# Gather stage: VectorE's segment scans of a tile are issued ahead of the add for the tile three places back

## The chip, the cores and the metric

The kernel runs on 1 core of one Trainium2 chip. The metric is the device time of one execution in microseconds; lower is better. The times shown are the median of three runs and one profiled execution.

## The reference, cut to what matters

Two graph layers, each followed by a residual and a layer norm, over 50,000 nodes of 256 numbers with 12,500 edges sorted by destination. Layer 0 is the one in which the changed code works:

```python
h = einsum('ni,hid->nhd', x, W)
e = leaky(sum(h[src]*a_src) + sum(h[dst]*a_dst))
alpha_norm = softmax of e over the edges that share a dst
msg = alpha_norm[:, :, None] * h[src]
out_h = segment_sum(msg, dst)
x = layernorm(x + out_h.reshape(N, H*D) @ W_out)
```

Layer 1 does the same kind of thing with queries, keys, values and a gate, and ends in a second layer norm. A node that no edge points to gets nothing from either sum, so the kernel sends all nodes through a cheap path and redoes only the rows that edges touch.

## The kernel before, in words

All five engines run one list of steps in the same order (`order_of`). The list is a blend of two kinds of steps: *node* steps, 196 of them, each for 256 nodes without edges (class `Nodes`), and the steps of the edge stages, which follow each other: `Score`, a softmax, `Gather`, `Message`, a second softmax, `Output`. Each engine walks this list alone and waits on semaphores, so the list fixes the order of the work within each engine and nothing else.

The change is in `Gather`. The 12,500 edges are 100 tiles of 125. For tile n:

- GpSimd multiplies the stored head rows by the softmax weights into `MSG` (L1212), in step n-3.
- TensorE transposes both halves of `MSG` into PSUM bank 5 (L1247), in step n. Bank 5 is single, so this waits until the scans of tile n-1 have read it (`scanned`).
- VectorE runs two segment scans over bank 5 into `AT` (L1280), in step n. A scan takes its carry from the last column of tile n-1.
- TensorE multiplies `AT` by the output weights, four matmuls into bank 6 or 7 by turns (L1254), in step n+2. A bank is free again when the add of two tiles before has read it, which is the wait on `z_ready`.
- VectorE adds the bank to the residual row in `ring` (L1271), in step n+3, and counts `z_ready`.
- SyncE stores the row (L1223), in step n+4, and loads the row of a tile four ahead (L1232), and once in five tiles a mask (L1726).

TensorE's two waits of a step, with t the step and n = t - 2, are these:

```python
pe.wait_ge(self.made, t + 1)
at_least(pe, self.scanned, t)
...
pe.wait_ge(self.scanned, n + 1)
at_least(pe, self.z_ready, n - 1)
```

In the list the Gather steps share the time with 66 node steps, by turns: mostly one or two Gather steps between two node steps. Two Gather steps with no node step between them are called a *pair* below. From tile 4 on there are 36 pairs whose both tiles are live, the first with tiles 4 and 5, the last with tiles 96 and 97; steps 99 and 100 are a further pair in which only step 99 has scans, and steps 101 and 102 one with none.

A node step on TensorE is four transposes (L741) and eight matmuls (L751). On VectorE it is L770, L777, L785 and, in every second node step, the normalisation L791; in the others a tiny L764 stands in front and ScalarE normalises (L722). The second and third part of the first softmax's weights (L1175, L1177 on VectorE) are put in the list behind Gather steps 3 and 10.

Of the kernel before, what the change touches and what calls it, by code (L numbers as in the profile page):

```python
# [23 lines left out]
ALU = mybir.AluOpType  # L24
# [6 lines left out]
N, D = 50000, 256  # L31
# [4 lines left out]
EDGES, TILES = 125, 100  # L36
# [13 lines left out]
def at_least(eng, sem, value):  # L50

    if value > 0:
        eng.wait_ge(sem, value)
# [24 lines left out]
def live(s, lag, total):  # L78

    return 0 <= s - lag < total  # L80
# [77 lines left out]
class Head:  # L158
# [73 lines left out]
    def vector(self, dve):  # L232
        w = self.c.scratch
        dve.memset(w.row[:, 0:2, :], 0.0).then_inc(self.dve_done, 1)
        dve.memset(w.row[:, 2, :], float(SKIP)).then_inc(self.dve_done, 1)
        dve.memset(w.previ, -1).then_inc(self.dve_done, 1)
        dve.memset(w.nexti, -1).then_inc(self.dve_done, 1)
        dve.memset(w.row[:, 3, :], 1.0).then_inc(self.dve_done, 1)
        dve.wait_ge(self.dve_done, 5)
        dve.wait_ge(self.idx_in, 32)  # L240
        dve.tensor_copy(w.row[:, 0, 1:1 + EDGES], w.srci).then_inc(self.dve_done, 1)
        dve.tensor_copy(w.row[:, 1, 1:1 + EDGES], w.dsti).then_inc(self.dve_done, 1)
        dve.tensor_copy(w.dstf, w.dsti).then_inc(self.dve_done, 1)
        dve.wait_ge(self.dve_done, 8)
        dve.wait_ge(self.columns, 3)
# [935 lines left out]
class Gather:  # L1181
# [81 lines left out]
    def vector(self, dve):  # L1263
        c, ps, R = self.c, self.c.psum, self.c.R

        def emit(t):
            if live(t, 3, TILES):
                n = t - 3
                dve.wait_ge(self.product, n + 1)
                dve.wait_ge(self.rows_in[n % R], 16 * (n // R + 1))  # L1270
                dve.tensor_tensor(c.ring[:, n % R, 0, :], ps[:, 6 + n % 2, 0:D], c.ring[:, n % R, 0, :], ALU.add).then_inc(self.z_ready, 1)  # L1271
            if live(t, 0, TILES):
                if t % G == 0:
                    dve.wait_ge(self.keeps[t // G % 2], 16 * (t // (2 * G) + 1))
                dve.wait_ge(self.turned, t + 1)
                at_least(dve, self.product, t - 3)
                at_least(dve, self.scanned, t)
                for h in range(2):
                    carry = c.AT[:, (t - 1) % 4, h * P + EDGES:h * P + EDGES + 1] if t > 0 else 0.0
                    last = dve.tensor_tensor_scan(c.AT[:, t % 4, h * P:(h + 1) * P], c.MB[:, t // G % 2, t % G, :], ps[:, 5, h * P:(h + 1) * P], carry, ALU.mult, ALU.add)  # L1280
                last.then_inc(self.scanned, 1)
        return emit


# [660 lines left out]
```

## Time and profile before

| what | us |
|---|---|
| median of 3 runs | 1260.95 |
| lowest and highest run | 1257.87, 1261.74 |
| profiled execution, time | 1271.05 |
| profiled execution, span of the core | 1269.3 |
| TensorE busy, share of the span | 93% |
| VectorE busy, share of the span | 82% |
| Gather stage, from 445 to 706 us | 261 |

The span runs from the first to the last instruction of the profiled execution. Busy times are sums of instruction durations on an engine. TensorE's durations overlap from one matmul to the next and their ends are modelled, so TensorE is best read by the starts of its groups.

### The profile page before, as it was taken

How to read it: one execution, taken by the hardware profiler on the slowest of the kernel's cores; microseconds unless marked ns; L12 is line 12 of the kernel's file. 1: busy time of each engine (PE TensorE's matmuls, PEld its weight loads, DVE VectorE, ACT ScalarE, POOL GpSimd, SP SyncE). 2: the span in 40 equal slices, each digit the busy share in tenths (PEclk: the TensorE clock that was granted, in tenths of full speed). 3: DMA queues.
4: the chain of work that ended last, by engine and by line, in shares of the span. 5: the costliest groups of instructions: out<-in, count | busy, mean ns of one | idle time of the engine just before them, and what ended most of it. 6: DMA issues, size and time to landing. Idle time of an engine off the chain costs nothing.

```text
span 1269.3 us, 28496 instructions
## 1 busy us (share of the span) xinstructions
PE 1174.8 (93%) x6990; PEld 1024.3 (81%) x6990; DVE 1041.8 (82%) x3799; ACT 829.2 (65%) x2787; POOL 851.0 (67%) x1076
## 2 busy tenths in 40 slices
PE   2899999999998689999999899999999996899995
PEld 2788999988896578788788699989999995688884
DVE  2767776777778799999999889999999987788985
ACT  0366666665666866666666856666665668689996
POOL 6688888888883455555554677767677743278887
PEclk9899999999999899999999999999999998899998
DMA  7578888888884477788877787777777742555652
GB/s 210 164 224 284 270 268 257 270 268 266 262 265 132 134 254 249 244 267 249 259 253 238 220 255 217 217 223 221 206 220 223 224 136 78 158 189 187 185 188 96
DMA packets 208795, 276.99 MB, mean 218 GB/s; under 512 B 40044, under 2 KB 140419, under 8 KB 208633
## 3 DMA queue, kind: packets, MB, share of 16 engines
q1 hardware_dynamic: 187913, 223.83, 56.0%
q0 software_dynamic: 19264, 50.85, 13.5%
q8 instruction: 60, 0.98, 0.3%
q14 instruction: 102, 0.84, 0.2%
q10 hardware_dynamic: 1456, 0.49, 0.2%
HBM read 159.67 MB, written 117.12 MB: 218 GB/s over the span
## 4 chain that ended last, share of the span: by engine, by line
PE 58%; DVE 17%; issue 12%; POOL 7%; ACT 3%; DMA 1%; another core or an unknown queue 1%; SPq 1%; DVEq 0%; POOLq 0%; ACTq 0%
PE banks L751 19%; PE banks L864 7%; PE banks L741 6%; PE banks L1422 4%; POOL out L1577 4%; PE banks L854 3%; PE banks L1254 3%; POOL output_r L1583 3%; DVE AT L1280 3%; PE banks L866 2%; PE banks L1409 2%; PE banks L1427 2%; PE banks L953 2%; PE banks L1247 2%; DVE node_X L777 2%
## 5 line engine op out<-in xcount | busy, mean ns | idle before, releaser
L751 PE MATMUL banks<-m_ext,node_XT 128*128 128x257 f32 x1568 | 376.0, 382 | 0.0
L751 PEld LDWEIGHTS banks<-m_ext,node_XT 128*128 128x128 f32 x1568 | 284.6, 192 | 33.0
L777 DVE SCALAR_TENSOR_TENSOR node_X<-banks,node_be,node_X 128x256 f32<-128x256 f32 x392 | 169.4, 474 | 79.5 <-ACT node_be L703 53.6
L678 POOL TENSOR_TENSOR node_r<-node_vv,half 128x4 f32<-128x4 f32 (+1 forms) x202 | 212.8, 1053 | 17.1 <-POOL node_vv L673 0.3
L709 ACT ACTIVATE node_XT<-banks 128x512 f32<-128x512 f32 x196 | 117.5, 599 | 131.7 <-PE banks L741 126.9
L673 POOL TENSOR_SCALAR node_vv<-node_mv 128x4 f32<-128x4 f32 (+1 forms) x202 | 56.5, 279 | 190.3 <-DVE node_mv L785 173.7
L716 ACT ACTIVATE node_sq<-node_X 128x256 f32<-128x256 f32 x392 | 158.0, 409 | 1.2 <-DVE node_X L777 1.2
L770 DVE BATCH_NORM_STATS2 node_st<-node_X 128x6 f32<-128x256 f32 x392 | 145.4, 412 | 1.3 <-issue 0.5
L690 ACT ACTIVATE node_X<-node_X,node_r 128x256 f32<-128x256 f32 x326 | 146.0, 497 | 0.0
L741 PE MATMUL banks<-ident,node_X 128*128 128x128 f32 x784 | 122.0, 279 | 19.0 <-issue 11.9
L831 POOL DMA_INDIRECT ring<-in_x,src_col x100 | 106.8, 1068 | 26.5 <-issue 14.4
L877 ACT ACTIVATE ST<-banks 128x512 f32<-128x512 f32 x100 | 59.8, 598 | 97.5 <-PE banks L854 40.1
L1345 POOL DMA_INDIRECT ring<-rows,src_pos x100 | 106.2, 1062 | 22.8 <-issue 19.7
L741 PEld LDWEIGHTS banks<-ident,node_X 128*128 128x128 f32 x784 | 95.7, 148 | 31.9 <-issue 16.4
L831 POOL DMA_INDIRECT ring<-in_x,dst_col x100 | 97.0, 970 | 31.4 <-issue 31.1
L1577 POOL DMA_INDIRECT out<-store,last_col x90 | 91.4, 1015 | 23.7 <-issue 23.4
L864 PE MATMUL banks<-wh,ST 128*128 128x260 f32 x400 | 105.9, 387 | 1.5 <-ACT store L886 0.2
L1622 PE MATMUL banks<-m_ext,AT 128*128 128x257 f32 x400 | 106.2, 388 | 0.7 <-ACT AT L1660 0.5
L1422 PE MATMUL banks<-w_kv,ST 128*128 128x256 f32 x400 | 105.0, 385 | 0.3 <-DVE store L1470 0.3
L1254 PE MATMUL banks<-wo,AT 128*128 128x256 f32 x400 | 103.0, 380 | 0.0
L1280 DVE TENSOR_TENSOR_SCAN AT<-MB,AT,banks 128x128 f32<-128x128 f32 x198 | 84.0, 466 | 20.2 <-PE banks L1247 17.1
L1449 ACT ACTIVATE ST<-banks 128x512 f32<-128x512 f32 x100 | 59.3, 593 | 62.9 <-PE banks L1409 54.9
(270 smaller groups left out, 2740.8 us busy)
## 6 DMA issues: line engine op xcount, KB each, us to landing
node_X<-in_x SPq DMA_DIRECT2D x196, 256.0 KB
out<-node_X SPq DMA_DIRECT2D x196, 256.0 KB
ring<-rows SPq DMA_DIRECT2D x210, 128.0 KB
rows<-ring SPq DMA_DIRECT2D x100, 256.0 KB
rows<-ring SPq DMA_DIRECT2D x200, 128.0 KB
MB<-keeps SPq DMA_DIRECT2D x40, 320.0 KB, 4.5
store<-rows SPq DMA_DIRECT2D x90, 128.0 KB
MB<-picks SPq DMA_DIRECT2D x50, 128.0 KB
```

Of the source, the lines that this page charges most:

```text
L678: pool.tensor_tensor(r[:, s % 4, NT * lo:NT * hi], v, self.c.half[:, NT * lo:NT * hi], ALU.pow).then_inc(self.roots, 1)
L690: last = eng.activation(row, row, ACT.Identity, scale=rz)
L716: last = act.activation(self.sq[:, k, :], X[:, n % U, k, :], ACT.Square, scale=1.0 / D ** 0.5, accum_out=self.mv[:, s % 4, 1, k, 1:2])
L741: last = pe.transpose(ps[:, 4, k * D + h * P:k * D + (h + 1) * P], self.X[:, n % U, k, h * P:(h + 1) * P], c.ident[:, :])
L751: last = pe.matmul(ps[:, NT * o + k, 0:D + 1], self.XT[:, o, k * D + h * P:k * D + (h + 1) * P], c.m_ext[:, h, :], start=(h == 0), stop=(h ...
L770: last = dve.bn_stats(st[:, s % 2, k, :], X[:, s % U, k, :])
L777: last = dve.scalar_tensor_tensor(out=X[:, n % U, k, :], in0=ps[:, b + k, 0:D], scalar=self.be[:, n % 4, k:k + 1], in1=X[:, n % U, k, :], ...
L831: pool.indirect_dma_start(out=c.ring[:, n % R, side, :], out_offset=None, in_=self.x, in_offset=bass.IndirectOffsetOnAxis(ap=col[:, n:n + ...
L864: pe.matmul(ps[:, 6, 0:HP], c.ST[:, o, h * P:(h + 1) * P], c.wh[:, h, :], start=(h == 0), stop=(h == 1))
L1254: last = pe.matmul(ps[:, 6 + n % 2, 0:D], c.AT[:, n % 4, h * P:(h + 1) * P], c.wo[:, h, :], start=(h == 0), stop=(h == 1))
L1422: pe.matmul(ps[:, 6, 0:2 * DM], c.ST[:, o, h * P:(h + 1) * P], c.w_kv[:, h, :], start=(h == 0), stop=(h == 1))
L1577: pool.indirect_dma_start(out=self.out, out_offset=bass.IndirectOffsetOnAxis(ap=c.last_col[:, n:n + 1], axis=0), in_=self.row(n), in_offse ...
```

## The change

In each Gather step VectorE issued the add for tile t-3 and then the two scans of tile t. Now it issues the scans of tile t and then the add for tile t-3. Waits go with their instructions. No other engine's code is touched, and no instruction is added or removed.

```diff
         def emit(t):
-            if live(t, 3, TILES):
-                n = t - 3
-                dve.wait_ge(self.product, n + 1)
-                dve.wait_ge(self.rows_in[n % R], 16 * (n // R + 1))
-                dve.tensor_tensor(c.ring[:, n % R, 0, :], ps[:, 6 + n % 2, 0:D], c.ring[:, n % R, 0, :], ALU.add).then_inc(self.z_ready, 1)
             if live(t, 0, TILES):
                 if t % G == 0:
                     dve.wait_ge(self.keeps[t // G % 2], 16 * (t // (2 * G) + 1))
...
                 last.then_inc(self.scanned, 1)
+            if live(t, 3, TILES):
+                n = t - 3
+                dve.wait_ge(self.product, n + 1)
+                dve.wait_ge(self.rows_in[n % R], 16 * (n // R + 1))
+                dve.tensor_tensor(c.ring[:, n % R, 0, :], ps[:, 6 + n % 2, 0:D], c.ring[:, n % R, 0, :], ALU.add).then_inc(self.z_ready, 1)
         return emit
```

## Rows read from the trace of the kernel before

**Rows 1.** Page, the span and busy time by engine, with share and instructions.

```profile
span 1269.3 us, 28496 instructions
...
PE 1174.8 (93%) x6990; PEld 1024.3 (81%) x6990; DVE 1041.8 (82%) x3799; ACT 829.2 (65%) x2787; POOL 851.0 (67%) x1076
```

**Rows 2.** Busy time by stretch: start:end and length, the engines, clock, DMA share, GB/s.

```profile
445.00:706.00 261.00, 251.36 (x1347) 209.21 (x1348) 239.65 (x773) 170.53 (x562) 137.01 (x221) 1.00 0.79 249
```

**Rows 3.** Waits from 445 to 706: us in total, times, longest us.

```profile
DVE AT L1280 <- PE banks L1247: 17.1, 59, 0.5
PE banks L1247 <- DVE AT L1280: 9.6, 37, 1.3
```

**Rows 4.** Timeline, 560 to 575: start, us, instruction, idle before and releaser.

```profile
567.46 0.38 PE L1247 MATMUL banks<-ident,MSG 128*128 128x128 f32 x2
567.88 0.85 DVE L1280 TENSOR_TENSOR_SCAN AT<-MB,AT,banks 128x128 f32<-128x128 f32 x2 [0.45 <-PE banks L1247]
568.55 0.60 PE L741 MATMUL banks<-ident,node_X 128*128 128x128 f32 x4
568.65 0.73 DVE L770 BATCH_NORM_STATS2 node_st<-node_X 128x6 f32<-128x256 f32 x2
570.72 0.38 PE L1247 MATMUL banks<-ident,MSG 128*128 128x128 f32 x2
570.85 0.42 DVE L1271 TENSOR_TENSOR ring<-banks,ring 128x256 f32<-128x256 f32 x1
571.18 0.84 DVE L1280 TENSOR_TENSOR_SCAN AT<-MB,AT,banks 128x128 f32<-128x128 f32 x2
572.01 0.42 DVE L1271 TENSOR_TENSOR ring<-banks,ring 128x256 f32<-128x256 f32 x1
572.17 0.41 PE L1247 MATMUL banks<-ident,MSG 128*128 128x128 f32 x2 [0.20 <-DVE AT L1280]
572.41 1.03 PE L1254 MATMUL banks<-wo,AT 128*128 128x256 f32 x4
572.67 0.85 DVE L1280 TENSOR_TENSOR_SCAN AT<-MB,AT,banks 128x128 f32<-128x128 f32 x2 [0.24 <-PE banks L1247]
573.28 0.60 PE L741 MATMUL banks<-ident,node_X 128*128 128x128 f32 x4
```

**Rows 5.** Timeline behind step 10, where the softmax part stands in VectorE's queue.

```profile
470.32 1.63 DVE L1175 RECIPROCAL scores<-scores 128x240 f32<-128x240 f32 x1
...
476.34 0.41 PE L1247 MATMUL banks<-ident,MSG 128*128 128x128 f32 x2 [1.26 <-DVE AT L1280]
```

**Rows 6.** Timeline, VectorE, scans and add in the first and last of 36 pairs.

```profile
453.54 0.84 DVE L1280 TENSOR_TENSOR_SCAN AT<-MB,AT,banks 128x128 f32<-128x128 f32 x2
454.30 0.40 DVE L1271 TENSOR_TENSOR ring<-banks,ring 128x256 f32<-128x256 f32 x1
...
692.41 0.85 DVE L1280 TENSOR_TENSOR_SCAN AT<-MB,AT,banks 128x128 f32<-128x128 f32 x2 [0.40 <-PE banks L1247]
693.27 0.42 DVE L1271 TENSOR_TENSOR ring<-banks,ring 128x256 f32<-128x256 f32 x1
```

**Rows 7.** Timeline near 1094, Output stage: matmuls that had waited for VectorE.

```profile
1093.85 0.48 DVE L1702 SCALAR_TENSOR_TENSOR ring<-banks,output_gates,ring 128x256 f32<-128x256 f32 x1
1094.45 0.73 PEld L1622 LDWEIGHTS banks<-m_ext,AT 128*128 128x128 f32 x4 [0.47 <-issue]
1094.48 1.11 PE L1622 MATMUL banks<-m_ext,AT 128*128 128x257 f32 x4 [0.26 <-DVE ring L1702]
1095.42 0.27 PE L1640 MATMUL banks<-ident,MSG 128*128 128x128 f32 x1
```

**Rows 8.** Timeline near 1050, Message stage: the same kind of wait.

```profile
1050.24 0.29 DVE L1470 TENSOR_TENSOR store<-banks,S 128x128 f32<-128x128 f32 x1 [2.63 <-ACT S L1456]
...
1050.63 1.10 PE L1422 MATMUL banks<-w_kv,ST 128*128 128x256 f32 x4 [0.34 <-DVE store L1470]
...
1051.57 0.38 PE L1423 MATMUL banks<-we,MB 128*128 128x128 f32 x2
```

**Rows 9.** Timeline, the end of the scans, steps 99 and 100.

```profile
700.17 1.89 PE L1254 MATMUL banks<-wo,AT 128*128 128x256 f32 x8
700.38 0.85 DVE L1280 TENSOR_TENSOR_SCAN AT<-MB,AT,banks 128x128 f32<-128x128 f32 x2 [0.43 <-PE banks L1247]
701.90 0.60 PE L741 MATMUL banks<-ident,node_X 128*128 128x128 f32 x4
```

**Rows 10.** SyncE's queue, waits from 445 to 706 us.

```profile
SPq L1223 <- DVE ring L1271: 46.3, 38, 3.4
```

**Rows 11.** DMA issues by line, 500 to 650: KB each, median us to landing.

```profile
MB<-keeps SPq DMA_DIRECT2D x11, 320.0 KB, 4.4
```

## The prediction, written before the result was known

> **What bounds the kernel now.** I began with the page [rows 1]: TensorE is busy for 93% of the span and VectorE for 82%, over stages that differ, so neither number says what the changed step is worth. The changed lines run only in the Gather stage, and I took the busy times of that stretch alone [rows 2]. In its 261 us TensorE is busy for 251.4 (96%) and VectorE for 239.7 (92%), at a granted clock of 1.00. Nearly everything that makes TensorE later there makes the stage longer.
>
> Then the waits of the stage [rows 3]. TensorE waits for one thing only: its transposes of MSG (L1247) for the scans (L1280), 37 times, 9.6 us in total. VectorE waits 59 times, 17.1 us, for those transposes. TensorE never waits at L1254, the matmul that needs the bank which the add empties. So z_ready is a wait that is always satisfied today.
>
> The timeline shows where the 37 waits are [rows 4]. A transpose at 567.46 belongs to a Gather step that stands alone between node steps. VectorE waits for it and starts the scans at 567.88, 0.42 later; TensorE goes on with the node step at 568.55 and loses nothing. The transposes at 570.72 and 572.17 are a pair. The second can't start before the scans at 571.18 have ended, at 572.02, and starts 0.15 behind them. A pair without any wait would take 1.09 us from transpose to transpose (567.46 to 568.55 is one step's work); it takes 1.45. Counting from the end e of the first tile's scans, the pair runs: second transposes e + 0.15, matmul L1254 e + 0.39, second scans e + 0.65, next node step on TensorE e + 1.26. The last figure is 1.25 to 1.27 in 31 of the 36 pairs.
>
> **The change part by part.** Nothing is added or removed: 100 adds of 0.41 and 100 pairs of scans change places. VectorE's busy time stays. What can move is who waits, and there are three questions.
>
> *Do the scans start earlier?* In a step that stands alone, no: they wait for TensorE already [rows 4], so there the add moves from an idle place to one behind the scans. In a pair behind a node step with the normalisation L791, VectorE is late and the add stands directly ahead of the scans (570.85, then 571.18), 0.33 us that seem to be gained. But the add of the step before now stands ahead of that node step. From scans to scans, 567.88 to 571.18, VectorE's work is scans 0.77, node step 2.20 (568.65 to 570.85), add 0.33, together 3.30; afterwards it is scans 0.77, add 0.33, node step 2.20, again 3.30. And the transposes at 570.72 wouldn't have let the scans start before 571.14. The gain per pair is 0; if the order did matter, 0.04. The stretch with the softmax part [rows 5] is the same case: until TensorE is released at 476.34 VectorE has the same work in another order.
>
> *Does TensorE get a new wait?* Yes, in each pair. In the second step t + 1 of a pair TensorE's matmul for tile t - 1 needs the add of tile t - 3. That add was issued ahead of the scans of tile t, for which the transposes had to wait anyhow. Now it is issued behind them. What I read as its new end is where the second add of a pair ends today, for it too follows the scans directly: 572.01 + 0.42 = 572.43, e + 0.41 [rows 4]; over the 36 pairs the median is 0.41, from 0.32 in the first pair to 0.45, with 0.43 in the last [rows 6]. The matmul would like to start at e + 0.39, and its weight load before that, so it waits.
>
> What a released group of four such matmuls costs must come from elsewhere, since L1254 has never waited. In the Output stage L1622, four matmuls of 257 columns, waits for an add of VectorE that ends at 1094.33; the weights start at 1094.45, the matmul at 1094.48, and what follows on TensorE at 1095.42, 1.09 after the release [rows 7]. In the Message stage the same is 1050.53 to 1051.57, 1.04 [rows 8]. The first has the same shape of wait (an add that reads PSUM and ends a bank's use), and I take 1.09. The node step behind a pair then starts at e + 0.41 + 1.09 = e + 1.50 in place of e + 1.26: **0.24 us per pair**. The bounds are 0.32 + 1.04 - 1.26 = 0.10 and 0.45 + 1.09 - 1.26 = 0.28. The second scans stay at e + 0.65, since the add ends before that, so nothing is won or lost there.
>
> The weights of the released group are loaded at 1094.45, 0.12 after the add's end and not before it [rows 7]. If they could be in place when the release comes, the group would run at the pace of an undisturbed one, 0.87 (572.41 to 573.28), from 0.15 behind the release (572.02 to 572.17): 0.41 + 0.15 + 0.87 - 1.26 = 0.17 per pair. The Trainium skill, "TensorE: Matmul & The Clock Gate", section "Architectural detail: the array is 16× 32×32, not 1× 128×128", says that TensorE's queue can pull weight loads ahead of matmuls in flight, which would make for the smaller price. The load at 1094.45 shows no such thing over a wait, so I keep 0.24.
>
> *How many, and do they add up?* There are 36 pairs. The one at steps 10 and 11 costs nothing, as TensorE afterwards stands 1.26 us for VectorE anyway [rows 5]. 35 x 0.24 = 8.4 us. They add, as the next step after each pair is paced by TensorE: its transposes come 2.17 behind the node step's start (568.55 to 570.72) and the scans 0.42 behind that, e + 1.50 + 2.17 + 0.42 = e + 4.09, while VectorE with the add now ahead of the node step is ready at e + 0.65 + 0.77 + 0.33 + 2.20 = e + 3.95 at the worst. Today these are e + 3.85 and e + 3.95. 13 pairs come directly after another pair's node step, and where that step holds L791, VectorE was the later one by up to 0.10, so part of the delay is hidden. With about half of them, 0.1 x 6 = 0.6 comes off; most second scans start at 0.60 rather than 0.65, and I take off 0.3.
>
> *The end.* Steps 99 and 100 have their eight matmuls back to back, from 700.17, with the node step at 701.90 [rows 9]. The four of step 100 need the add of tile 96, which now follows the scans that end at 701.23: 701.23 + 0.41 + 1.09 = 702.73, 0.83 later than today, once. Steps 101 and 102 have no scans.
>
> *Other engines.* SyncE waits 38 times for the add before it stores the row [rows 10], and behind the store in its queue are the row load, the mask load and the node steps' transfers. All of these go out later by the scans, about 0.8 us. The loads are issued four node steps (some 16 us) or four tiles (some 10 us) ahead, and a mask takes 4.4 us to land [rows 11]: hidden. If that cover were gone, it would be one shift of 0.8 us, not one per tile, as the queue keeps its pace. GpSimd and ScalarE wait for no add.
>
> Sum: 8.4 - 0.3 + 0.83 = 8.9 us on the profiled execution's span of 1269.3 (its time is 1271.05), 0.7%. That execution is 10.1 us slower than the median of the runs shown, 1260.95, and I assume the same 8.9 there: **1269.9 us**. A change of 0.3%, 3.8 us, is about what a measurement of this kernel can tell from none.
>
> **The rivals.**
>
> *Faster: the scans were held by the add.* If VectorE were late by the whole add in every pair behind an L791, with no add taking its place ahead of the node step, some 20 pairs would each gain 0.33, 6.6 us: 1254.4. For it speaks the order of 570.85 and 571.18, and 9.6 us of TensorE waiting for scans. Against it, the same 3.30 us of work either way, and the transposes that allow 0.04. It decides only if the matmul's wait is also satisfied by e + 0.27, that is an add end at e + 0.15, and the earliest seen is 0.32. Chance 0.07.
>
> *No change: the new wait is absorbed.* If VectorE and not TensorE sets when the next scans of a pair start, a delay of TensorE up to its slack is given back. I found up to 0.10 of such slack, and in pairs after pairs only; a run without profiling might have more. With all pairs at the lower bound, 35 x 0.10 + 0.5 = 4 us is still at the edge of what can be told. If two thirds of the 8.9 are absorbed: 1264. Chance 0.13.
>
> *Slower than forecast: SyncE's late queue.* If transfers of the node steps or masks lose their cover in places, VectorE stands at L770 or L1280. By the 0.8 us it would have to happen several times, each behind a fresh catching up: five times is 4 us, 1274. SyncE has had waits of up to 3.4 us for the add [rows 10] without anyone waiting for a load. Chance 0.08.
>
> *Slower by less: the released group loses no pace.* At 0.17 per pair and 701.23 + 0.41 + 0.15 + 0.87 - 701.90 = 0.76 at the end, the sum is 35 x 0.17 - 0.3 + 0.76 = 6.4: 1267.4. Against it stand both rows of released groups [rows 7, 8], whose groups take longer than an undisturbed one: 1094.48 to 1095.42 and 1050.63 to 1051.57 are 0.94 each. Chance 0.07. The rule cited above would lead here.
>
> *My forecast,* 35 new waits of 0.10 to 0.28, has the remaining 0.65.
>
> **How the numbers follow.** The bounds give 35 x 0.10 + 0.5 = 4 and 35 x 0.28 + 0.9 = 10.7 us: 1265 to 1271.7. The measurement itself moves by 2 or 3 us (1257.87 to 1261.74 in three runs), and the upper rival reaches to 1274. The range 1264 to 1274 leaves out the faster rival and part of the absorbed case below, and little above. Slower by over 0.3%: the forecast, the smaller price and the upper rival, 0.80, with 0.02 from the absorbed case at its edge, make 0.82. Within 0.3%: 0.11. Faster: 0.07.
>
> **What the changed profile would show.** The waits of the stage would have a new row, L1254 for the add L1271, some 36 times with about 0.1 us each, and perhaps 0.5 at the end. The transposes L1247 wait for the scans as often as before and for about the same total. In the timeline of a pair the node step stands at e + 1.50, not 1.26; the scans, at most 0.04 earlier. The stage lasts about 270 us in place of 261, with TensorE's busy share a little lower. VectorE's idle time ahead of the scans grows. I would be wrong if the L1247 wait shrank by several us, if L1254 never waited, or if the node steps stood later but the stage didn't.

## The result

| kernel | median us | runs |
|---|---|---|
| before | 1259.45 (1256.98 to 1261.74) | 20 |
| changed | 1264.86 (1261.68 to 1266.97) | 20 |

The ratio is 1.0036, with a 95% interval of 1.0028 to 1.0045: the changed kernel is 3.5 to 5.7 us slower. The direction was forecast and the time lies in the range, but the loss was forecast at 8.9 us; the medians differ by 5.4 us, and 1.0036 is 4.5 us, about half of the forecast.

The two profiled executions can't be compared by their spans: the changed kernel's is 1260.4 us, 8.9 us *shorter* than the kernel before's 1269.3 [rows 1]. The first transposes of MSG begin at 441.0 us in one and at 431.2 in the other, and up to there the two kernels run the same instructions; in the other nine profiles of this document they begin at 429.8 to 432.8 us, so it is the kernel before's profile that stands out. Behind the stage the changed kernel's profile is 4.3 us shorter too (559.9 us for 564.2), at a granted clock of 0.98 for 0.97. So I compare the stage: from the first transposes of MSG to the start of the last add. The page of the changed kernel, its span and engines:

```profile
span 1260.4 us, 28496 instructions
...
PE 1172.6 (93%) x6990; PEld 1019.6 (81%) x6990; DVE 1041.0 (83%) x3799; ACT 835.3 (66%) x2787; POOL 851.2 (68%) x1076
```

Busy time by stretch, kernel before, from the first transposes to the last add (columns as in [rows 2]):

```profile
441.00:705.10 264.10, 253.41 (x1359) 210.59 (x1358) 241.26 (x775) 174.11 (x573) 139.31 (x226) 1.00 0.79 250
```

The same stretch of the changed kernel:

```profile
431.20:700.50 269.30, 258.48 (x1359) 211.44 (x1358) 240.65 (x775) 174.29 (x573) 141.32 (x226) 1.00 0.79 246
```

The stage is 5.2 us longer, which lies within the 3.5 to 5.7 us that the times give: it is as large as the whole loss. VectorE's busy time is the same to 0.6 us (240.65 for 241.26). The waits from 435 to 700 us in the changed kernel, the answer to [rows 3]:

```profile
DVE AT L1275 <- PE banks L1247: 21.7, 57, 0.6
PE banks L1247 <- DVE AT L1275: 9.2, 37, 1.3
...
PE banks L1254 <- DVE ring L1281: 0.5, 1, 0.5
```

TensorE's waits hardly moved, and the new wait shows once only, with 0.5 us. The waits within the 36 pairs are not in this view: TensorE's busy time grew by 5.1 us instead. A group of two transposes is shown as 0.41 us long, with a modelled end, and the matmul that waits starts before that end. So the wait is read from the starts. The timeline of the changed kernel, the answer to [rows 4]:

```profile
559.65 0.38 PE L1247 MATMUL banks<-ident,MSG 128*128 128x128 f32 x2
560.07 0.85 DVE L1275 TENSOR_TENSOR_SCAN AT<-MB,AT,banks 128x128 f32<-128x128 f32 x2 [0.57 <-PE banks L1247]
560.84 0.40 DVE L1281 TENSOR_TENSOR ring<-banks,ring 128x256 f32<-128x256 f32 x1
...
562.91 0.38 PE L1247 MATMUL banks<-ident,MSG 128*128 128x128 f32 x2
563.37 0.84 DVE L1275 TENSOR_TENSOR_SCAN AT<-MB,AT,banks 128x128 f32<-128x128 f32 x2
564.13 0.40 DVE L1281 TENSOR_TENSOR ring<-banks,ring 128x256 f32<-128x256 f32 x1
564.36 0.41 PE L1247 MATMUL banks<-ident,MSG 128*128 128x128 f32 x2 [0.20 <-DVE AT L1275]
564.64 0.73 PEld L1254 LDWEIGHTS banks<-wo,AT 128*128 128x128 f32 x4
564.67 1.10 PE L1254 MATMUL banks<-wo,AT 128*128 128x256 f32 x4
564.86 0.85 DVE L1275 TENSOR_TENSOR_SCAN AT<-MB,AT,banks 128x128 f32<-128x128 f32 x2 [0.33 <-PE banks L1247]
565.61 0.60 PE L741 MATMUL banks<-ident,node_X 128*128 128x128 f32 x4
```

With e = 563.37 + 0.84 = 564.21: transposes e + 0.15, as before; add from e - 0.08 to e + 0.32; the matmul's weight load e + 0.43; matmul e + 0.46 in place of 0.39; node step e + 1.40 in place of 1.26. In all 36 pairs the node step stands at 1.40 or 1.41 behind e. From scans to scans over the node step it is 560.07 to 563.37, 3.30 us, as before (567.88 to 571.18): the add has moved across the node step and gained nothing.

The first and the last pair of the changed kernel on VectorE, the answer to [rows 6]; in both the add ends at e + 0.32:

```profile
443.76 0.84 DVE L1275 TENSOR_TENSOR_SCAN AT<-MB,AT,banks 128x128 f32<-128x128 f32 x2
444.52 0.40 DVE L1281 TENSOR_TENSOR ring<-banks,ring 128x256 f32<-128x256 f32 x1
...
686.90 0.85 DVE L1275 TENSOR_TENSOR_SCAN AT<-MB,AT,banks 128x128 f32<-128x128 f32 x2 [0.52 <-PE banks L1247]
687.67 0.40 DVE L1281 TENSOR_TENSOR ring<-banks,ring 128x256 f32<-128x256 f32 x1
```

Behind the softmax part [rows 5] TensorE still stands, 0.15 less, since that pair's new delay is taken out of this wait. And the end, the answer to [rows 9]: without the wait the group at 696.33 would have started at 695.68, 0.87 behind the one at 694.81.

```profile
466.84 0.41 PE L1247 MATMUL banks<-ident,MSG 128*128 128x128 f32 x2 [1.11 <-DVE AT L1275]
...
694.81 1.03 PE L1254 MATMUL banks<-wo,AT 128*128 128x256 f32 x4
696.33 1.10 PE L1254 MATMUL banks<-wo,AT 128*128 128x256 f32 x4 [0.49 <-DVE ring L1281]
697.27 0.60 PE L741 MATMUL banks<-ident,node_X 128*128 128x128 f32 x4
```

The node step stands 2.46 behind the matmuls' start in place of 1.73 [rows 9]: 0.73 us. SyncE's queue in the changed kernel waits longer for the add, the answer to [rows 10]:

```profile
SPq L1223 <- DVE ring L1281: 77.7, 50, 3.3
```

**Why the add ends earlier than I read.** In the kernel before the second add of a pair, which I took as the model, is not paced by the scans. It needs the matmul group of the first step of the same pair. Two more lines of the kernel before, that group in the pair of [rows 4] and the first transposes of the last pair:

```profile
570.94 1.03 PE L1254 MATMUL banks<-wo,AT 128*128 128x256 f32 x4
...
691.99 0.38 PE L1247 MATMUL banks<-ident,MSG 128*128 128x128 f32 x2
```

The group ends at 571.97, and the add starts at 572.01 [rows 4], 0.04 behind it. Counted from the first transposes of the pair, the add ends at 572.43 - 570.72 = 1.71 [rows 4], and in the last pair at 693.69 - 691.99 = 1.70 [rows 6], though the scans start 0.46 behind the transposes in one and 0.42 in the other. It is 1.71 in 33 of the 36 pairs, while e lies anywhere from 1.27 to 1.35 behind the transposes. In the pairs at steps 4 and 12, whose scans start 1.59 and 1.51 behind the transposes, the group was long done and the add followed the scans at once, to e + 0.32; in the pair at step 10 the softmax part stands ahead of it. The changed kernel's add is for a tile one place older, whose matmuls are long done, so it always follows at once. 0.32 was the lower bound of my range and should have been the value.

### The profile page after: what moved, and what is told of

It reads as the page before. It is cut to its first block, busy times and chain, and to the rows that moved or that the text cites. A ratio compares the mean times of both kernels' runs of the same rounds, so it can differ in the third digit from the quotient of the medians.

```text
span 1260.4 us, 28496 instructions
## 1 busy us (share of the span) xinstructions
PE 1172.6 (93%) x6990; PEld 1019.6 (81%) x6990; DVE 1041.0 (83%) x3799; ACT 835.3 (66%) x2787; POOL 851.2 (68%) x1076
## 4 chain that ended last, share of the span: by engine, by line
PE 59%; DVE 15%; issue 12%; POOL 7%; ACT 4%; DMA 1%; SPq 1%; DVEq 0%; POOLq 0%; ACTq 0%
PE banks L751 20%; PE banks L864 7%; PE banks L741 6%; PE banks L1422 5%; POOL out L1577 4%; PE banks L1254 4%; PE banks L854 3%; POOL output_r L1583 3%; PE banks L866 2%; DVE AT L1275 2%; PE banks L1409 2%; PE banks L1427 2%; PE banks L953 2%; PE banks L1247 2%; DVE node_st L770 2%
## 5 line engine op out<-in xcount | busy, mean ns | idle before, releaser
L1254 PE MATMUL banks<-wo,AT 128*128 128x256 f32 x400 | 105.6, 386 | 0.5 <-DVE ring L1281 0.5
L1275 DVE TENSOR_TENSOR_SCAN AT<-MB,AT,banks 128x128 f32<-128x128 f32 x198 | 84.1, 466 | 25.8 <-PE banks L1247 21.7
```

The costliest lines, as they stand in the source:

```text
L1254: last = pe.matmul(ps[:, 6 + n % 2, 0:D], c.AT[:, n % 4, h * P:(h + 1) * P], c.wo[:, h, :], start=(h == 0), stop=(h == 1))
```

## The experiments

All ratios are to the kernel before, run beside each on the same chip, with 5 to 10 runs of each experiment. Its median is 1261.09 us beside strict, firsts, notfirsts and lag3, and 1260.77 beside the others; the row of the changed kernel is the one above. The stage is measured as above, from each profile's own first transposes to its last add.

| kernel | ratio, 95% interval | stage us |
|---|---|---|
| before | 1 | 264.1 |
| changed | 1.0036 [1.0028, 1.0045] | 269.3 |
| lag3 | 1.0028 [1.0016, 1.0039] | 266.9 |
| firsts | 1.0023 [1.0011, 1.0035] | 268.6 |
| notfirsts | 1.0062 [1.0048, 1.0076] | 271.6 |
| strict | 1.0070 [1.0057, 1.0084] | 273.9 |
| matfirst | 0.9953 [0.9940, 0.9966] | 257.5 |
| matfirst_after | 1.0258 [1.0244, 1.0271] | 297.5 |
| splate | 1.0005 [0.9994, 1.0016] | 264.1 |
| end99 | 1.0036 [1.0023, 1.0049] | 268.6 |

### strict: the wait that I had priced

```diff
 # kernel before, TensorE; seconds: the second steps of pairs
-                at_least(pe, self.z_ready, n - 1)
+                at_least(pe, self.z_ready, n if t in self.seconds else n - 1)
```

> The kernel before with one wait made stricter: in the second step of a pair the matmul L1254 waits for the add of that same step, which follows the scans of the first and ends at e + 0.41 where the changed kernel's add ends at e + 0.32. This is the wait that the prediction priced. Theory (the price is the add's end + 1.08 - 1.26): 0.23 per pair, node step at e + 1.49, 35 x 0.23 + 0.8 = 9 us, ratio 1.0065 to 1.0075. Rival (a fixed price for any such wait, or a loss that the rest of the stage partly gives back): the same as the changed kernel, 1.003 to 1.005.

Measured 1270.27 us to 1261.09, 1.0070, stage + 9.8. The timeline of strict, a pair with e = 567.79:

```profile
566.95 0.84 DVE L1280 TENSOR_TENSOR_SCAN AT<-MB,AT,banks 128x128 f32<-128x128 f32 x2
567.78 0.42 DVE L1271 TENSOR_TENSOR ring<-banks,ring 128x256 f32<-128x256 f32 x1
...
568.35 1.10 PE L1254 MATMUL banks<-wo,AT 128*128 128x256 f32 x4
569.29 0.60 PE L741 MATMUL banks<-ident,node_X 128*128 128x128 f32 x4
```

The add ends at e + 0.41, the matmul starts at e + 0.56 and the node step at e + 1.50. Over the pairs the add's end runs from e + 0.31 to e + 0.45, but for the pair at steps 10 and 11, and the node step follows it at 1.08 to 1.09 throughout. In that one pair the stricter wait is for an add behind the softmax part, which ends at e + 2.32; by the starts of the transposes this costs 1.1 us that neither the prediction nor the changed kernel has. The other 8.7 us of the stage stand against the 8.9 that I had priced. So the price of a release was right, the pairs add up nearly without loss, and something close to 8.9 us would have been the answer if the add had ended where I put it. The rival of a fixed price is out.

### firsts: the new order in the first steps of pairs only

```diff
 # changed kernel, VectorE; add(t) is the add for tile t - 3
+            ahead = t not in self.firsts
+            if ahead: add(t)
...
+            if not ahead: add(t)
```

> The new order in the first step of each pair only, the old one in all other steps. Theory: the whole loss is there, the ratio is that of the changed kernel, 1.003 to 1.005, and the pairs show the node step at e + 1.40. Rival 1 (later node steps on VectorE or later stores over all steps are the cause): two thirds of the steps have the old order, so about a third of the loss, 1.001 to 1.002. Rival 2 (the add ahead of the scans held them): VectorE has no add between the scans of a lone step and those of a pair behind a node step, 2.97 us of work in place of 3.30, so the pairs behind a node step with L791 gain 0.33 each, some 6 us, which would undo the loss; my theory allows 0.04 each, as the transposes come then.

Measured 1264.61 us to 1261.09. The stage is 4.5 us longer, against 5.2 in the changed kernel, and its pairs have the node step at e + 1.40. So nearly all of the loss comes from 37 of the 97 steps that have both an add and scans. The ratio of 1.0023 is below the 1.003 that I had expected at least, and the time's interval, 1.4 to 4.4 us, reaches down to my first rival; the stage doesn't. Rival 2, a gain of 0.33 in pairs behind L791, is out but for the pair at step 4, where the scans stood 1.59 behind their transposes and now stand 1.25. In 26 of the pairs the scans now start 0.42 behind their transposes, with VectorE idle ahead of them, and can't start sooner; the pair of [rows 4] had 0.46. The timeline of firsts:

```profile
563.52 0.38 PE L1247 MATMUL banks<-ident,MSG 128*128 128x128 f32 x2
...
563.94 0.85 DVE L1285 TENSOR_TENSOR_SCAN AT<-MB,AT,banks 128x128 f32<-128x128 f32 x2 [0.21 <-PE banks L1247]
```

### notfirsts: the new order in all other steps

```diff
 # firsts, VectorE
-            ahead = t not in self.firsts
+            ahead = t in self.firsts
```

> The old order in the first step of each pair, the new one in all other steps. No matmul waits for an add. Theory: between the scans of a step and the scans of a pair behind a node step with L791, VectorE now has two adds: 0.77 + 0.33 + 2.20 + 0.33 = 3.63 us in place of 3.30, against transposes that are ready at 3.26, so each of about 19 such pairs loses 0.33 to 0.38 us: 6 to 7 us, ratio 1.004 to 1.006, with the first scans of those pairs 0.8 us or more behind their transposes. Rival 1 (any step in the new order costs through later stores or node steps): about two thirds of the changed kernel's loss, 3 us, 1.002 to 1.003. Rival 2 (the add ahead of the scans costs nothing since VectorE has slack): no change.

Measured 1268.25 us to 1261.09, stage + 7.5. No matmul waits for an add here (node steps at e + 1.26). The loss is the second add between two scans, as the timeline of notfirsts shows: 560.93 to 564.55 is 3.62 us, and the scans start 0.78 behind transposes that began at 563.77. The stage's 7.5 us are more than the 6 to 7 expected, because nine further pairs, with their scans 0.60 behind the transposes, lose about 0.16 each.

```profile
560.93 0.85 DVE L1285 TENSOR_TENSOR_SCAN AT<-MB,AT,banks 128x128 f32<-128x128 f32 x2 [0.43 <-PE banks L1247]
561.70 0.40 DVE L1271 TENSOR_TENSOR ring<-banks,ring 128x256 f32<-128x256 f32 x1
...
564.22 0.42 DVE L1271 TENSOR_TENSOR ring<-banks,ring 128x256 f32<-128x256 f32 x1
564.55 0.84 DVE L1285 TENSOR_TENSOR_SCAN AT<-MB,AT,banks 128x128 f32<-128x128 f32 x2
```

VectorE's work between two scans does set the pace in these places. It is the same 3.30 in the kernel before and in the changed one, which is why moving all the adds gained nothing.

### lag3: the new order without the wait

```diff
 # changed kernel, TensorE
-            if live(t, 2, TILES):
-                n = t - 2
+            if live(t, 3, TILES):
+                n = t - 3
```

> The changed order on VectorE, and TensorE's matmuls L1254 issued one Gather step later (tile t-3 in step t in place of t-2). The matmul in the second step of a pair then needs an add of the step before the pair, so the new wait is gone while VectorE keeps the new order. Theory (the matmul of a pair's second tile waits for the add that now follows the scans, 0.14 us per pair): the node step behind a pair stands at e + 1.26 again and the time is that of the kernel before plus at most 1 us for the one step more at the end, ratio 0.999 to 1.001. Rival 1 (VectorE's node steps or SyncE's stores being later is the cause): the time stays where the changed kernel is, ratio 1.003 to 1.005.

The expectation of no loss failed: 1264.98 us to 1261.09. In the trace the wait is gone, with node steps at e + 1.26 in all pairs, and the stage is 2.8 us longer, not 5.2. The edit brought costs of its own that I had missed: the add now needs matmuls of its own step, so in a lone step it waits for them, as the timeline of lag3 shows.

```profile
560.58 0.85 DVE L1275 TENSOR_TENSOR_SCAN AT<-MB,AT,banks 128x128 f32<-128x128 f32 x2 [0.31 <-PE banks L1247]
561.44 0.42 DVE L1281 TENSOR_TENSOR ring<-banks,ring 128x256 f32<-128x256 f32 x1
...
564.00 0.84 DVE L1275 TENSOR_TENSOR_SCAN AT<-MB,AT,banks 128x128 f32<-128x128 f32 x2
```

Here the add starts 0.01 behind the scans' end, where it starts 0.08 ahead of it in the changed kernel, and scans to scans take 3.42 us in place of 3.30, for some 19 pairs about 2 us; and the one step more at the end has the last add wait for eight matmuls, near 0.9 us. Summed over the stage, the starts of the transposes give 1.8 us up to the last ones, and 0.9 come behind them, so these two account for the 2.8. By the time alone lag3 can't be told from the changed kernel, so it shows the wait gone, and not cleanly what it cost.

### splate: SyncE's queue late by itself

```diff
 # kernel before, SyncE
-                sp.wait_ge(self.z_ready, n + 1)
+                sp.wait_ge(self.z_ready, min(n + 2, TILES))
```

> The kernel before, with SyncE's store of a row waiting for the add of one tile later, which makes SyncE's whole queue about 2.5 us later, three times the 0.8 us by which the change delays it. Theory (SyncE's queue is covered): no change, ratio 0.999 to 1.001. Rival 1 (the late queue is part of the changed kernel's loss): at least 1.002.

Measured 1260.59 us to 1260.77, and a stage of 264.1 us, to the tenth that of the kernel before. SyncE waits more than in the changed kernel:

```profile
SPq L1223 <- DVE ring L1271: 98.5, 94, 3.4
```

The interval of 0.9994 to 1.0016 leaves out the 1.002 of the rival. SyncE's queue is covered; the upper rival of the prediction has no part in the loss.

### end99: the old order in step 99 alone

```diff
 # firsts, VectorE
-            ahead = t not in self.firsts
+            ahead = t == 99
```

> The changed kernel with the old order in step 99 alone, the last step with scans, whose pair partner has a matmul group but no transposes. Theory: the group of step 100 no longer waits (0.49 us of idle time in the changed kernel), and the stage ends 0.72 us earlier than in the changed kernel; the rest of the loss stays, ratio 1.0025 to 1.0045. From the time alone this can't be told; it is read from the trace of the last steps.

Measured 1265.21 us to 1260.77. In the trace the eight matmuls stand back to back again and the node step is 1.73 behind their start; the stage is 268.6 us, 0.7 shorter than in the changed kernel.

```profile
693.40 1.89 PE L1254 MATMUL banks<-wo,AT 128*128 128x256 f32 x8
695.13 0.60 PE L741 MATMUL banks<-ident,node_X 128*128 128x128 f32 x4
```

### matfirst and matfirst_after: TensorE's order in a pair

```diff
 # TensorE; product(t) is the matmul group for tile t - 2
+            if t in self.seconds:
+                product(t)
...
+            if t not in self.seconds:
+                product(t)
```

> The kernel before (old order on VectorE), with TensorE's matmul L1254 issued ahead of the transposes L1247 in the second step of each pair. Theory (in a pair TensorE stands idle 0.36 us for the scans while a matmul group of 0.87 us, whose operands and bank are ready, is queued behind the transposes): the group fills the idle time, transpose to transpose in a pair becomes 1.95 us, the node step comes 0.21 behind it, 2.16 behind the first transposes in place of 2.53, 0.37 less per pair and 13 us in all: ratio 0.988 to 0.992, if VectorE keeps up; its second scans move 0.5 us later and its work per pair stays. Rival (VectorE at 92% of the stage is as much the bound): the scans slip behind and the gain is under a third, ratio 0.997 to 1.0.

> The same edit on TensorE, on the changed kernel (scans ahead of the add). Theory: the matmul that is now ahead of the second transposes needs the add that follows the first scans, so it starts at e + 0.46, the transposes at e + 1.40 and the node step at e + 1.61 in place of 1.26 in the kernel before: 0.35 x 35 = 12 us slower than before, ratio 1.009 to 1.013, some 25 us between the two orders. Rival (the order of add and scans matters little, TensorE's wait is a matter of 0.1 us): near the first kernel of this pair, ratio below 1.0.

matfirst is the kernel before with this edit, and beats both: 1255.22 us to 1260.77, and its stage is 6.6 us shorter. The timeline of matfirst, a pair:

```profile
558.33 0.38 PE L1258 MATMUL banks<-ident,MSG 128*128 128x128 f32 x2
558.55 1.89 PE L1248 MATMUL banks<-wo,AT 128*128 128x256 f32 x8
560.28 0.38 PE L1258 MATMUL banks<-ident,MSG 128*128 128x128 f32 x2
560.50 0.60 PE L741 MATMUL banks<-ident,node_X 128*128 128x128 f32 x4
```

The node step stands 2.17 behind the first transposes, as worked out, where it was 2.56 (570.72 to 573.28 in [rows 4]). The ratio 0.9953 lies between the two expectations: of the 13 us about half arrived in the stage. VectorE doesn't keep up in every pair, and the matmul waits for an add that is late because VectorE is. The waits of TensorE in matfirst from 431 to 700 us:

```profile
PE banks L1248 <- DVE ring L1277: 4.0, 8, 1.4
PE banks L741 <- issue: 2.6, 4, 0.8
PE banks L1258 <- DVE AT L1286: 0.3, 1, 0.3
```

The wait for the scans, 9.6 us in [rows 3], is down to 0.3. The missing 6 us are in the starts of the node steps. In 16 of the 36 pairs the node step is not 2.17 but 2.41 to 2.76 behind the first transposes, which adds up to 5.9 us. A late pair of matfirst:

```profile
537.59 0.38 PE L1258 MATMUL banks<-ident,MSG 128*128 128x128 f32 x2
538.31 0.39 DVE L1277 TENSOR_TENSOR ring<-banks,ring 128x256 f32<-128x256 f32 x1
540.00 0.60 PE L741 MATMUL banks<-ident,node_X 128*128 128x128 f32 x4
```

VectorE reaches the add of the pair's first step 0.72 behind the transposes, its end at 538.70 releases the second matmul group, and the node step stands 2.41 behind the transposes.

With the scans ahead of the add, the same edit costs 32 us: 1293.19 to 1260.77. I had expected 12. The waits of matfirst_after from 445 to 695 us:

```profile
PE banks L1248 <- DVE ring L1287: 32.2, 33, 2.5
```

I had taken the scans to start 0.42 behind the first transposes in every pair. In the trace VectorE starts them 0.7 to 1.4 us behind the transposes in 33 of the 36 pairs, so the matmul waits about 1 us for the add that follows them; that this lateness feeds on itself from pair to pair is my reading, and no run isolates it. The order of add and scans decides here between a gain of 5.5 us and a loss of 32.

## Where the prediction was right, and the step that failed

- *The stage is bound by TensorE and everything adds up:* right. strict puts 0.24 us on average into each of 35 pairs and 1.1 into one, and gets 9.8 us of stage.
- *The scans gain nothing:* right. 3.30 us between scans in both orders; notfirsts shows what two adds there would cost, firsts that taking one away is worth 0.04 (0.42 for 0.46), and 0.33 only in the one pair whose scans were far behind.
- *The new wait is at L1254 in each pair:* right. The matmul starts at e + 0.46 in place of e + 0.39 in all 36 pairs of the changed kernel, and the node step is back at e + 1.26 in lag3 and notfirsts.
- *The price of a release, 1.09:* right. 1.40 - 0.32 = 1.08, and the same in strict.
- *The add's end at e + 0.41:* wrong, and this is the step that failed. "What I read as its new end is where the second add of a pair ends today, for it too follows the scans directly": it doesn't; it waits for the matmuls of the pair's first step. The changed kernel's add waits for nothing but the scans and ends at e + 0.32. The price per pair is 0.14 and not 0.24, and the term is 35 x 0.14 = 4.9 us in place of 8.4.
- *The end of the stage:* 0.73 for 0.83, off by nearly the same 0.1.
- *Pairs directly after pairs give back 0.3:* right in kind, 0.2 in size. In five such pairs the scans come 0.03 to 0.08 sooner behind their transposes than in the kernel before. 4.9 + 0.7 = 5.6 against 5.2 measured leaves 0.4. The rest of that, up to 0.3, is none of the change's doing: in five pairs of the kernel before's profile the node step already stood at e + 1.29 to e + 1.37, where splate, with the same order, has e + 1.26 in all of them.
- *SyncE's queue is covered:* right, by splate.
- *The weight loads aren't ahead of the wait:* the slower rival of 0.17 per pair was built on the same e + 0.41. With 0.32 and an unchanged pace it would give 0.08 per pair, and the trace has 0.14. In all 36 pairs of the changed kernel the load starts 0.12 behind the add's end and the matmul 0.03 behind that, as in [rows 7].
- *What would show:* the new row of 36 waits did not appear, as the modelled end of the transposes covers all of them and only the one at the end of the stage shows. TensorE's busy share of the stage didn't fall either (96% in both). VectorE's wait for the transposes grew as forecast, from 17.1 to 21.7 us.

With the right end of the add the prediction's own sum is 4.9 - 0.3 + 0.73 = 5.3 us. The medians differ by 5.4; that the two agree so closely is partly luck, as the interval is 3.5 to 5.7.

## What to carry to other kernels

When an instruction is moved behind another, its new end is that of the other plus its own length, less what the two overlap (here 0.40 - 0.08 = 0.32), unless a wait of its own is later. Take the model for it from an instance whose waits are all long satisfied; here the instance read from the trace followed the scans by eye, but its end was fixed 1.71 us behind the transposes, and one look at three pairs by that measure would have shown it.

On an engine that runs one list over and over, moving an instruction across its neighbour in every step left the engine's own pace as it was here (3.30 us in both orders), and changed it only for those that wait for the two. Where only some steps were changed (notfirsts), or the moved add got a wait of its own (lag3), the pace did change. Ask for each waiter whether it had slack, and look first for idle time in which a queued instruction with ready operands could run: that edit was worth 5.5 us here.

## What the runs showed of the hardware

A short wait between two matmul groups doesn't show as idle time in this profile: neither the 0.07 us of the changed kernel (matmul at e + 0.46 for e + 0.39) nor strict's 0.17 (e + 0.56). In the changed kernel's stage TensorE's busy time rises by 5.1 us with the same instructions and the same clock, and the idle time by 0.1. A released group of four matmuls is shown as 1.10 us and an undisturbed one as 1.03, and the next group starts 0.94 and 0.87 behind it, in all 36 pairs of the changed kernel and all of strict's: a release costs 0.07 us of pace beyond the wait. The weights of a released group are loaded 0.03 us ahead of its first matmul (564.64 and 564.67), and those of an undisturbed one 0.11 ahead in 32 of the kernel before's 37 pairs, the one at step 2 counted in.
